# Value and output biases as 33-row products in existing PSUM sums, epsilon through VectorE's aggregate, in a four-stage transformer kernel

## The reference, cut

```python
h = tok(x)                                   # patches @ W.T + b, class token, position table
h = h + gate_scan(layernorm(layernorm(h)))   # sigmoid gate, linear recurrence over tokens; eps 1e-5 twice
h = h + ffn(layernorm(h))                    # ternary W_fc, gelu, layernorm(h)*ln_w+ln_b, ternary W_proj
# attention of layer 1
y = layernorm(h)
Q, K = rope(y @ Wq.T + bq), rope(y @ Wk.T + bk)
V = y @ Wv.T + bv
A = softmax(causal(Q @ K.T / sqrt(C)))
h = h + (A @ V) @ Wf.T + bf
# ffn of layer 1
y = layernorm(h)
x_int = clip(round(y / scale), -127, 127)
h = h + (x_int * scale) @ (ternary_weight - 1).T + bias
```

## Time and profile before

| | us |
|---|---|
| median of 3 runs | 163.69 (163.63 to 164.32) |
| the profiled execution, its own time | 163.71 |
| its span, first to last instruction | 161.9 |
| busy: PE / DVE / POOL / ACT | 148.2 / 136.1 / 120.3 / 109.0 |
| longest work groups on POOL: power / variance plus epsilon | 33.3 / 24.2 |
| DMA, mean over the span | 67 GB/s |

### The profile page before, as it was taken

One profiled execution on the slowest core, in us unless ns is written; L12 is line 12 of the kernel. 1 busy time (PEld: TensorE's weight loads), 2 busy tenths in 40 slices (PEclk: granted clock), 3 DMA queues, 4 the chain that ended last, 5 costly groups with the idle time before them and its releaser, 6 DMA issues.

```text
span 161.9 us, 3532 instructions
## 1 busy us (share of the span) xinstructions
PE 148.2 (91%) x1043; PEld 129.5 (80%) x1043; DVE 136.1 (84%) x396; ACT 109.0 (67%) x264; POOL 120.3 (74%) x214
## 2 busy tenths in 40 slices
PE   7979999999998999999999999999999999697541
PEld 7969999788997887879888989988998798574220
DVE  0767679999999999999979799888988896896871
ACT  3765359736448899999998958498827637276330
POOL 1068978968927466878889988869899888988830
PEclk9999999999999999999999999999999999999955
DMA  5999992000030000000000000000000000001323
GB/s 171 340 392 392 379 417 109 4 0 2 0 130 4 2 0 2 0 4 0 0 4 2 0 4 0 2 0 0 4 0 0 0 6 2 2 10 46 87 81 81
DMA packets 6026, 10.84 MB, mean 67 GB/s; under 512 B 1841, under 2 KB 3448, under 8 KB 5752
## 3 DMA queue, kind: packets, MB, share of 16 engines
q1 hardware_dynamic: 6008, 10.62, 18.7%
HBM read 9.40 MB, written 1.21 MB: 66 GB/s over the span
## 4 chain that ended last, share of the span: by engine, by line
PE 70%; POOL 13%; DVE 6%; issue 6%; ACT 2%; DVEq 0%; ACTq 0%; POOLq 0%
PE bank L428 37%; PE bank L508 5%; PE bank L575 5%; PE bank L509 4%; PE bank L510 4%; PE bank L517 3%; POOL small L1186 3%; PE bank L435 3%; POOL qk L1251 2%; POOL small L1181 2%; POOL residual L1282 2%; POOL small L1191 2%; PE bank L549 1%; PE bank L629 1%; DVE residual L1160 1%
## 5 line engine op out<-in xcount | busy, mean ns | idle before, releaser
L1186 POOL TENSOR_TENSOR small<-small,powers 111x1 f32<-111x1 f32 (+3 forms) x55 | 33.3, 606 | 3.7
L1181 POOL TENSOR_SCALAR small<-small 111x1 f32<-111x1 f32 (+1 forms) x55 | 24.2, 441 | 15.0 <-DVE small L892 11.3
L428 PE MATMUL bank<-pj,gt_hi 128*111 128x256 f32 (+1 forms) x88 | 22.3, 293 | 0.0
L428 PE MATMUL bank<-pj,gt_lo 128*111 128x256 f32 (+1 forms) x88 | 21.3, 281 | 0.0
L1202 POOL TENSOR_TENSOR x_lo<-x_raw,x_hi 128x666 fp32r<-128x666 f32 (+1 forms) x9 | 12.8, 1434 | 10.8 <-ACT x_hi L721 10.8
L508 PE MATMUL bank<-wt_hi,x_hi 128*111 128x256 f32 (+1 forms) x66 | 19.4, 294 | 1.4 <-DVE h L998 1.1
L510 PE MATMUL bank<-wt_hi,x_lo 128*111 128x256 f32 (+1 forms) x66 | 18.6, 282 | 0.0
L509 PE MATMUL bank<-wt_lo,x_hi 128*111 128x256 f32 (+1 forms) x66 | 18.6, 282 | 0.0
L428 PE MATMUL bank<-fc,n1t_hi 128*111 128x512 f16 (+1 forms) x44 | 16.7, 380 | 0.0
L428 PE MATMUL bank<-fc,n1t_lo 128*111 128x512 f16 (+1 forms) x44 | 16.6, 378 | 0.0
L428 PEld LDWEIGHTS bank<-pj,gt_hi 128*111 128x111 f32 (+1 forms) x88 | 15.1, 171 | 0.3 <-DVE residual L1088 0.2
(11 more groups left out here) (139 smaller groups left out, 478.9 us busy)
## 6 DMA issues: line engine op xcount, KB each, us to landing
x_raw<-x_in SPq DMA_DIRECT2D x10, 333.0 KB, 6.4
w_fc<-w_fc_in SPq DMA_DIRECT2D x1, 1024.0 KB, 10.2
w_pj<-w_pj_in SPq DMA_DIRECT2D x1, 1024.0 KB, 12.2
out_dram<-residual SPq DMA_DIRECT2D x10, 96.0 KB, 1.7
w_tok<-w_tok_in SPq DMA_DIRECT2D x2, 384.0 KB, 4.1
w_gate<-w_gate_in SPq DMA_DIRECT2D x1, 512.0 KB, 5.8
w_qk<-w_qk_in SPq DMA_DIRECT2D x1, 512.0 KB, 7.0
ln_w<-ln_w_in SPq DMA_DIRECT2D x1, 512.0 KB, 3.5
```

Of the source, the lines that this page charges most:

```text
L428: last = mm(out, a, b, start=(n == 0), stop=(n == len(pairs) - 1))
L1181: return nc.gpsimd.tensor_scalar(small[0:rows(i), i, out:out + 1], small[0:rows(i), i, value:value + 1], factor, add, ALU.mult, ALU.add)
L1186: return gt(small[0:rows(i), i, r:r + n], small[0:rows(i), i, ve:ve + n], powers[0:rows(i), 0:n], ALU.pow)
```

## The change

1. Bias rows as products. A matrix `pick` (33 rows, rows 0 and 32 all ones, the others zero) is multiplied with `value_rows` or `out_rows`: 33 copies of the bias row, of which row 0 is its fp32r high part and row 32 the rest. This product is the first of each of the 11 value sums and of each of the 11 out sums. The out bias is divided by the scale before (`w_out_bias`, new on POOL), since DVE multiplies the out sum with it. `vbias` and `biased` on POOL and the waits of DVE's attend and out for them are gone.
2. Epsilon. The statistics get a third group of three numbers (count 0, mean 0, a sum of squares of 256 epsilon), filled once; bn_aggr over 9 numbers gives the variance plus epsilon. Norm 0 has a fourth group and two aggregates per tile, one for each epsilon; a factor from its second normalisation goes into gamma (`w_gamma`). The 55 `scaled` steps on POOL are gone.
3. POOL's shift for norm 3 no longer waits for r times 1/scale but multiplies by -1/scale itself; ACT's n3 waits for both.
4. `ORDER` is a new table for all four engines. The position product is now PE's first after the warm-up products.

```diff
+STACK = 33
-        warm:0 tok:0 w_pos:0 tok:1 tok:2 tok:3 w_gate:0 tok:4 t0:0 tok:5 t0:1 tok:6 t0:2 tok:7 w_fold:0 t0:3
+        warm:0 w_pos:0 tok:0 tok:1 tok:2 tok:3 w_gate:0 tok:4 t0:0 tok:5 t0:1 tok:6 w_fold:0 tok:7 t0:2 tok:8
...
-            load(value_bias[:, :], bf_in.partition_broadcast(128), s["dma_vbias"])
-            load(out_bias[:, :], out_bias_in.partition_broadcast(128), s["dma_bias"])
+            load(value_raw[0:STACK, :], bf_in.partition_broadcast(STACK), s["dma_vbias"])
+            load(out_raw[0:STACK, :], out_bias_in.partition_broadcast(STACK), s["dma_bias"])
...
             def value_(i):
-                pairs = []
+                pairs = [(pick[0:STACK, 0:rows(i)], value_rows[0:STACK, :])]
...
             def out_(i):
+                mm(out[0:n, 0:D], pick[0:STACK, 0:n], out_rows[0:STACK, :], start=True, stop=False)
                 for k in range(KD):
-                    last = mm(out[0:n, 0:D], q3t[:, k, span(i)], w_out[:, k, :], start=(k == 0), stop=(k == KD - 1))
+                    last = mm(out[0:n, 0:D], q3t[:, k, span(i)], w_out[:, k, :], start=False, stop=(k == KD - 1))
...
             def mean_of(norm):
-                    nc.vector.bn_aggr(col(i, normed[norm][2], 2), stats[0:rows(i), norm, i % 2, 0:6])\
-                        .then_inc(s[f"mv{norm}_ready"], 1)
+                    groups = stats[0:rows(i), norm, i % 2, :]
+                    if norm == 0:
+                        nc.vector.bn_aggr(col(i, MV0_SQ, 2), groups[:, 0:3 * GROUP]).then_inc(s["mv0_ready"], 1)
+                        nc.vector.bn_aggr(col(i, MV0, 2), groups[:, 0:4 * GROUP]).then_inc(s["mv0_ready"], 1)
+                    else:
+                        nc.vector.bn_aggr(col(i, normed[norm][2], 2), groups[:, 0:3 * GROUP])\
+                            .then_inc(s[f"mv{norm}_ready"], 1)
...
             def w_ones(_i):
                 nc.vector.memset(ones[:, :], 1.0).then_inc(s["ones_ready"], 1)
+                nc.vector.memset(pick[0:STACK, :].bitcast(F32), 0.0).then_inc(s["pick_ready"], 1)
+                dve.wait_ge(s["pick_ready"], 1)
+                for r in (0, STACK - 1):
+                    nc.vector.memset(pick[r:r + 1, :].bitcast(F32), 1.0).then_inc(s["pick_ready"], 1)
...
             def w_value_bias(_i):
-                tt(value_bias[0:TILE, :], narrow(("value_bias", 0), TILE), value_bias[0:TILE, :], ALU.add)\
+                dve.wait_ge(s["pe_fold"], KD)
+                tt(value_bias[0:STACK, :], narrow(("value_bias", 0), STACK), value_raw[0:STACK, :], ALU.add)\
                     .then_inc(s["value_bias_ready"], 1)
+                dve.wait_ge(s["value_bias_ready"], 1)
+                nc.vector.tensor_copy(value_rows[0:STACK, :], value_bias[0:STACK, :]).then_inc(s["value_rows_ready"], 1)
+                dve.wait_ge(s["value_rows_ready"], 1)
+                lo = slice(STACK - 1, STACK)
+                low_part(value_rows[lo, :], value_bias[lo, :], value_rows[lo, :].bitcast(F32), s["value_rows_ready"])
...
             def attend(i):
-                dve.wait_ge(s["vbias_ready"], i + 1)
...
             def out_(i):
-                dve.wait_ge(s["biased_ready"], i + 1)
...
             def h0_(i):
-                pool.wait_ge(s["mv0_ready"], i + 1)
-                scaled(i, VE0, MV0 + 1, 1.0, LN_EPS).then_inc(s["ve0_ready"], 1)
-                scaled(i, VE0 + 1, MV0 + 1, 1.0 + LN_EPS, LN_EPS * LN_EPS).then_inc(s["ve0_ready"], 1)
-                pool.wait_ge(s["ve0_ready"], 2 * i + 2)
-                power(i, VE0, R0, 2).then_inc(s["r0_ready"], 1)
+                pool.wait_ge(s["mv0_ready"], 2 * i + 2)
+                power(i, MV0, R0, 2).then_inc(s["r0_ready"], 1)
...
             def attend(i):
                 pool.wait_ge(s["mv3_ready"], i + 1)
-                scaled(i, VE3, MV3 + 1, 1.0, LN_EPS).then_inc(s["ve3_ready"], 1)
-                pool.wait_ge(s["ve3_ready"], i + 1)
-                power(i, VE3, R3).then_inc(s["r3_ready"], 1)
+                power(i, MV3, R3).then_inc(s["r3_ready"], 1)
...
-                pool.wait_ge(s["rq_ready"], i + 1)
-                shift(i, NB3, MV3, RQ, "nb3_ready")
-
-            def biased(i):
-                n = rows(i)
-                pool.wait_ge(s["s3_ready"], i + 1)
                 if i == 0:
-                    pool.wait_ge(s["dma_bias"], 16)
-                gt(res[0:n, i, :], res[0:n, i, :], out_bias[0:n, :], ALU.add).then_inc(s["biased_ready"], 1)
+                    pool.wait_ge(s["neg_inv_scale_ready"], 1)
+                nc.gpsimd.tensor_scalar(small[0:rows(i), i, NB3:NB3 + 1], small[0:rows(i), i, MV3:MV3 + 1],
+                                        small[0:rows(i), i, R3:R3 + 1],
+                                        derived[0:rows(i), D_NEG_INV_SCALE:D_NEG_INV_SCALE + 1], ALU.mult,
+                                        ALU.mult).then_inc(s["nb3_ready"], 1)
+
+            def w_out_bias(_i):
+                out, bias = out_rows[0:STACK, :], out_bias[0:STACK, :]
+                pool.wait_ge(s["dma_bias"], 16)
+                pool.wait_ge(s["h0_ready"], TILES)
+                pool.wait_ge(s["inv_scale_ready"], 1)
...
```

More of the change, by code:

```diff
@@ new lines @@
+        tg:12 tg:13 fc:18 qk:0 t1:10 qk:1 qk:2 tg:14 tg:15 proj:6 qk:3 t2:4 proj:7 tg:16 fc:19 tg:17 fc:20 t2:5
+        value:0 t2:6 score:0 fc:21 score:1 t2:7 proj:8 tg:18 tg:19 qk:4 tg:20 qk:5 turn:0 score:2 proj:9 tg:21
+        qk:6 score:3 attend:0 qk:7 turn:1 value:1 proj:10 t2:8 turn:2 attend:1 value:2 value:3 attend:2 t2:9
+        score:4 turn:3 value:4 score:5 t2:10 turn:4 score:6 attend:3 qk:8 qk:9 value:5 attend:4 qk:10 score:7
+        turn:5 qk:11 value:6 turn:6 value:7 attend:5 turn:7 t3:0 attend:6 attend:7 t3:1 value:8 score:8 score:9
@@ L304, in tower @@
     w_out = m.own("w_out", [KD, D], F16)
-    pos_rows = m.own("pos_rows", [D], F32)
-    value_bias = m.own("value_bias", [D], F32)
+    pos_at = m.region(row)
+    pos_rows = m.at("pos_rows", [D], F32, pos_at)
+    out_bias = m.at("out_bias", [D], F32, pos_at)
+    rows_at = m.region(row)
+    value_rows = m.at("value_rows", [D], F32R, rows_at)
+    value_raw = m.at("value_raw", [D], F32, rows_at)
+    value_bias = m.at("value_bias", [D], F32, early + 7 * row)
     ln_bias = m.own("ln_bias", [D], F32)
-    out_bias = m.own("out_bias", [D], F32)
+    rows_at = m.region(row)
+    out_rows = m.at("out_rows", [D], F32R, rows_at)
+    out_raw = m.at("out_raw", [D], F32, rows_at)
+    pick = m.own("pick", [112], F32R)
     ones = m.own("ones", [128], F32)
@@ L467, in w_value_bias @@
                 for k in range(KD):
-                    last = mm(out[0:TILE, 0:D], packed[:, BIAS_V + k:BIAS_V + k + 1].to_broadcast([128, TILE]),
+                    last = mm(out[0:STACK, 0:D], packed[:, BIAS_V + k:BIAS_V + k + 1].to_broadcast([128, STACK]),
                               w_ft[:, k, :], start=(k == 0), stop=(k == KD - 1))
@@ L1178, in _, with power @@
             gt = nc.gpsimd.tensor_tensor
-            def scaled(i, out, value, factor, add):
-                return nc.gpsimd.tensor_scalar(small[0:rows(i), i, out:out + 1], small[0:rows(i), i, value:value + 1],
-                                               factor, add, ALU.mult, ALU.add)
-            def power(i, ve, r, n=1):
-                return gt(small[0:rows(i), i, r:r + n], small[0:rows(i), i, ve:ve + n], powers[0:rows(i), 0:n],
+            def power(i, mv, r, n=1):
+                return gt(small[0:rows(i), i, r:r + n], small[0:rows(i), i, mv + 1:mv + 2 * n:2], powers[0:rows(i), 0:n],
                           ALU.pow)
```

185 lines of the change are left out of this document (101 added, 84 removed).

## The result

The change made the kernel slower: 168.11 us median against 164.0 for the kernel before in the same session, ratio 1.0235 with an interval of 1.0176 to 1.0294. Medians in the text are of all executions of a kernel, while the ratios, and the table behind e14, leave out the ones that ran in the chip's slower state (here one of four, 170.7; the other three are 167.36, 167.68 and 168.53, some 3.9 us above before). The forecast was 160.7, range 157.9 to 163.6. The profiled execution took 167.68 us, span 165.9.

The account below looks back on a forecast made before the run. PE's order of products was taken as the clock until 136 us, DVE's own work as what is late next in the end. End -3.5, products +0.4, DVE 0, start +0.1: -3.0, so 160.7 us, range 157.9 to 163.6.

Parts of the forecast that it names:

- The 33-row products: On PE, 22 added bias products at 0.12 us each; with work moved behind qk:11, +0.4 us in the sum.
- The +0.7 before last qk: On PE, six value bias products before the last score-projection product add 0.7 us; bounds 0 and +2.5.
- the 0.2 in the end: In the end stretch, the bias product in each out sum adds one pitch to the last one: 0.2 us.
- rival (d): On PE, a 33-row product breaks the stream and costs 0.42 us: +2.1, 165.8 us; chance 0.06.
- The start: Before tok:1: tok:0 begins 1.3 us later behind DVE's wt_lo, yet tok:1 comes only 0.1 us later.
- The bound of 0.9: At the start, if the position table lands only at 9.05, everything behind it is 0.9 us later.
- rival (e): At the start, PE idles and its clock halves; products cost about twice 0.12 us, 2.7 for 22: 163.4 us; chance 0.04.
- The end stretch: From the last score-projection product to DVE's last instruction: 23.2 us becomes 19.7, so -3.5; bounds -4.5 and -1.1.
- POOL then no longer ends last: Before 154.0, POOL has 5.9 us less in a run of 13.6, so DVE ends last.
- No clip over 0.4 us: Sign expected after the change: DVE's clips no longer stand beside POOL additions, none over 0.4 us.
- DVE from 10.8 to 60: DVE's added 2.8 us is offset by 2.6 us of relief, rounded to 0; bounds -1.0 and +2.8.
- POOL's relief: On POOL, epsilon and bias additions go, leaving it near 82 us busy instead of 120.3.

Follow-up runs that it names:

- e14: Bias rows alone changed (128 rows), epsilon added on POOL as before, under the new order table with the start's order of before: 166.82 us.
- e3: The changed kernel with bias products on 128 rows and the start's order of before on PE and DVE: 159.98 us, ratio 0.975 to the kernel before.
- e1: The changed kernel with bias products on 128 rows (added rows zero in pick), order untouched: 162.3 us, ratio 0.989 to the kernel before.
- e15: e1 with 20 warm-up products instead of 11: 160.9 us, ratio 0.982 to the kernel before.
- e2: The changed kernel with the start's order of before on PE and DVE, bias products untouched: 166.46 us, ratio 1.016 to the kernel before.
- e9: All parts, 128-row products, order table of before, as e6 but with the out bias rows' three POOL instructions behind hc:0: 165.89 us.
- e13: Epsilon part alone, both biases added on POOL, under the new order table with the start's order of before: 166.38 us, ratio 1.012.
- e12: e3 with one more aggregate for each tile of norm 0 on DVE, result unused: 160.4 us, ratio 0.978 to the kernel before.
- e8: The kernel before with epsilon alone changed, both biases added on POOL and order as before: 164.96 us, ratio 1.005.
- e6: All parts of the change with 128-row bias products under the table of before, out bias rows behind h0:10 on POOL: 168.04 us, ratio 1.026.
- e11: e3 with the out bias rows on POOL behind hc:0 instead of between h0:7 and h0:8: 163.41 us, ratio 0.996 to the kernel before.

## Why the prediction was wrong, point by point

From the changed kernel to e3, 168.1 to 160.0: 5.8 us by the rows of the bias product (e1), 1.4 by the clock at the start (e15), 0.9 by the start's lateness (e3). In the other order the start is 1.7 (e2) and the rows are 6.5. The forecast of 160.7 fits the kernel without these two faults; it missed both.

**The 33-row products: the step that failed.** "I take 0.12, for it has the same type and columns as the neighbours in its own sum." The type and columns were right and the rows decided. On 96 and 128 rows it costs 0.12 to 0.2, on 33 and 64 rows 0.3 to 0.5 with what goes lost ahead and behind. The +0.7 before last qk was +2.6 by e2 against e3 (0.7 + 1.9; the middle as a whole grew by 1.6, since the rest of the change had taken a little from it), and the 0.2 in the end was over 4. Both bounds were on the page, 0 and 0.42, and I took the near one. The sentence of rival (d), "Against it: the load of its weights can run beside the product before, as for all others", is the premise that fell: the PEld rows show that it can't. The position product was the only row with few rows of the array, and I read it for its length alone. Rival (d) with 0.06 was the mechanism; its threshold of 0.26 us was passed.

The runs show a step between 64 and 96 rows (between 64 and 74, if the transpositions count), and each dear product costs at both sides. The Trainium skill (TensorEngine Tiling (Array Packing), Key Properties and Available Configurations) has a rule that bears on it: changing the tiling mode drains TensorE, and the modes have tiles of 128, 64 or 32 rows. The page doesn't say that a plain product on few rows, for which the kernel asks no tile, changes the mode; that it does is my reading. By it 33 rows would be a product in the 64-row mode between two in the full one, so two drains each, and 96 rows would stay in the full mode. The intervals fit: 0.30 on 33 and on 64 rows, 0.12 on 96 and 128, no such cost for transpositions on 74 and 111 rows. No trace shows the mode itself. It is a rule against this change that I should have weighed. The one I cited of the Trainium skill, that a load goes by columns whatever the contraction (TensorE: Matmul & The Clock Gate, LDWEIGHTS), holds as well: the loads take 0.17 us on 33 rows and on 128. It was not what the product cost.

**The start: +0.1 was +2.5 in the trace, 1.7 (e2) to 2.3 (e1 to e3) in time.** The bound of 0.9 took the table's landing to shift the rest by its own lateness, with the table there at 9.05; it was there at 8.49, sooner, and still tok:1 came 2.5 late. The working had tok:0 wait for DVE only ("begins 1.3 us later"); the wait for DMA, 2.39 us in one piece, was longer, and with it came rival (e): the granted clock dropped. (e) had it at 0.04, with 0.12 us more for each of 22 products, 2.7 us; measured are products of tok:0 (in e1's profile also the first of tok:1) at 0.21 instead of 0.12, 1.4 us. The prediction had said that the trace shows the drop at its end only; now it shows one at the start.

**The end stretch: -3.5 right in size, the reason half wrong.** In e1 it is 19.0, in e3 19.4, forecast 19.7; in the kernel after the dear products took it all back (23.1). But the working put it on POOL: "POOL then no longer ends last". e9 has that relief, and its end is 22.6, 0.6 less than before. The 3 us came with the order: ACT's last exponential 2.8 us sooner. The prediction had this as "ACT now takes the last exponential behind n3:5 instead of n3:7", among the reasons for 2.4 us. Of POOL's relief the end needs the bias additions gone and not the epsilon steps: e14 still has those and its end is 19.0. e13 keeps the additions and has 22.0, in an execution that I read for no more than that. So neither order nor relief is the cause by itself. "No clip over 0.4 us" was wrong for one of 11 (0.91).

**DVE from 10.8 to 60: 0, right in sum; the terms were not separated.** The threshold of w_fc took 1.54 us (3.15 before), and one more aggregate for each tile costs some 0.4 or nothing (e12). Aggregates of 9 and 12 numbers take 0.17 to 0.19 us, those of 6 took 0.17. From tok:1 to last qk e3 needs 124.95 us with six more products, before 125.2. Under the table of before the epsilon part alone makes this stretch 0.9 us longer (e8), so the 0 holds for the new table.

**POOL's relief** was 30 us busy, not 38 (120.3 to 82): the power became longer (mean 0.64 us for one column, 0.98 for two) and the out bias' scaling took 3.67 us. At these places neither shows in PE's waits; the out bias rows at another place do (e6, e11).

**The chances.** Slower had 0.08. (d) and (e) were counted as alternatives to each other; both happened, and they are independent of the gain, so their prices had to be added to it: -3.0 + 6.0 + 2.2 = +5.2 against +4.1 measured (the 2.2 is the start's 2.3 less the forecast's 0.1; e3, without both faults, was also 0.7 under the forecast).

## What to carry to other kernels

A matrix product that replaces work on an idle engine is only as cheap as its place in PE's stream: look whether its weight load runs beside the product ahead, and give it as many rows as its neighbours have, with zeros if need be (the 22 products filled up with zeros cost nothing that could be measured here; on 33 rows they cost 6 us). Put a product whose input comes late by DMA behind work that is ready, or fill the wait: PE pays the wait once and then the lower clock. In a kernel whose order is written out, test a part and its table together, and look what three instructions do in front of one power: over 3 us here.
